# AdaLN-FFN with LoRA experts on one core: the last tile's 656 columns as 236 and 420 instead of 144 and twice 256

## The chip, the cores and the metric

The kernel runs on one core of a Trainium2 chip. The metric is device time in microseconds of one execution, as the median over several runs; less is better. TensorE is called PE below, with its weight loads as PEld; VectorE is DVE, ScalarE ACT, GpSimd POOL and SyncE SP, whose queue issues the loads and stores.

## What is computed

`x` is (64, 32, 512): 64 items of 32 channels by 512 features. Each item picks one of 16 matrices (32 x 32) that mixes its channels, `y`; a linear layer of 512 to 512 with bias follows, with a LoRA delta of the two best of 8 experts, 16 ranks each:

```python
y = einsum('bct,bcd->bdt', x, weights[condition])
result = y @ W_base.T + b_base
logits = y @ W_gate.T                      # 8 experts
route_w = the two largest of softmax(logits), over their sum, at their places, else 0
h = einsum('bnd,erd->bner', y, A)          # 8 experts x 16 ranks
delta = einsum('bner,eor->bno', h * route_w[..., None], B)
out = x + result + delta
```

## The kernel before

**Tiles.** Four items make a tile of 128 rows; there are 16 tiles, 0 to 15 (`LAST`). `x_sb` holds all of them, and each tile's result is added into `x_sb` and stored from there.

**Splitting.** Each fp32 operand is held as a high and a low part, so one product is made of three: `y_hi` with `w_hi`, `y_hi` with `w_lo`, `y_lo` with `w_hi`. With four chunks of 128 features this gives twelve steps for each tile (`ORDER`). The weight side `w_all` has 648 columns: 256 of the base, 64 ranks, 256 of the base, 64 ranks, 8 of the gate. `BASE` is 256, `H` 64, `HALF` 320, `E` 8. The `y` part is the stationary operand and is loaded anew before every product.

**A middle tile** on PE: `mix_tile` (L461, the channel mix of the next tile), then twelve times two products of 320 and 328 columns into the two banks of `main_ps` (`main_step`, L479). Between them stand, for the tile before it, the transpose of `hw`, the weighted ranks (`turn`, L489), and six LoRA products (`lora`, L499).

**The last tile** has no successor to cover its routing. So PE first makes ranks and gate alone: `side_columns` takes 72 + 72 = 144 columns in two runs, twelve products into `y_ps[0]` (L554), and DVE can route (`route_tile`, L356 to L380) while PE makes the base's 512 columns, twelve times two products of 256 (L560). After step 1 stands `turn(14)`, after step 7 `turn(15)` and `lora(14)`. Then comes `lora(15, by_half=True)`: three products for the first half of the columns, then three for the second, each with a signal `base_done`.

**DVE in the last tile** goes in the written order: routing of tile 14, which ends in its `hw` (L376), routing of tile 15, `low_hwT(14)` (L385, the low part of the transposed ranks), the bias of tile 14 (L392), `low_hwT(15)`, the bias of tile 15, the add of tile 14 (L398), then two adds of 256 columns for tile 15 (L442). PE's `lora(t)` waits for `low_hwT(t)`, and its `turn(t)` for `hw` of `t`. ACT makes `hwT_hi` (L279) between the transpose and `low_hwT`.

**SP** issues each tile's store after its add (L209), and for tile 15 two stores of 128 x 256 (L213). At the end it waits for all of them.

Of the kernel before, what the change touches and what calls it, by code (L numbers as in the profile page):

```python
# [5 lines left out]
def adaln_ffn_kernel(  # L6
# [20 lines left out]
    ALU = mybir.AluOpType  # L27
# [9 lines left out]
    E = w_all.shape[1] - D - RANKS  # L37
# [6 lines left out]
    BASE, H, G = OUT // 2, RANKS // 2, E // 2  # L44
    HALF = BASE + H
    ALL = 2 * HALF + E
    SIDE = H + E
    LAST = TILES - 1
# [4 lines left out]
    STEPS = len(ORDER)  # L53
    TURN_AT, LORA_AT = 4, 9
    FIRST_MIX_AT = 6
    LAST_TURN_AT = 1, 7


    WARM_BEFORE, WARM_BESIDE, WARM_BEHIND = (512, 512, 512, 256), (256,), (256, 256, 256)
# [2 lines left out]
    out_tiles = out.rearrange("(t q) c n -> t (q c) n", q=Q)  # L62
# [3 lines left out]
    with ctx:  # L66
# [9 lines left out]
        x_sb = sb("x_sb", [P, TILES, D])  # L76
# [4 lines left out]
        b_hi = sb("b_hi", [P, OUT], f32r)  # L81
        b_lo = sb("b_lo", [P, OUT], f32r)
# [23 lines left out]
        hwT_hi = [sb(f"hwT_hi{i}", [P, P], f32r) for i in range(2)]  # L106
        hwT_lo = [sb(f"hwT_lo{i}", [P, P], f32r) for i in range(2)]
# [9 lines left out]
        y_ps = [ps(f"y_ps{i}") for i in range(2)]  # L117
        main_ps = [ctx.enter_context(nc.psum_tensor(f"main_ps{i}", [P, 2, 512], f32)) for i in range(2)]
# [52 lines left out]
        hwT_lo_ready = sem("hwT_lo_ready")  # L171
        base_done = sem("base_done")
# [3 lines left out]
        def first_halves():  # L176

            for h, bank in enumerate((y_ps[0], hwT_ps[0])):
                f = slice(h * D // 2, (h + 1) * D // 2)
                yield bank[:, 0:D // 2], y_hi[0][:, f], y_lo[0][:, f]  # L180

        block = ctx.enter_context(nc.Block())

        @block.sync
        def _(sp):
            def load_x(t):
                sp.dma_start(x_sb[:, t, :], x_tiles[t, :, :]).then_inc(x_landed[t], 16)

            def load_w(c):
                sp.dma_start(w_raw[:, c, :], w_chunks[c, :, :]).then_inc(w_landed[c], 16)  # L190

            sp.dma_start(cond_sb[:, :], cond).then_inc(cond_landed, 16)
            sp.dma_start(table[:, :, :], cond_w.rearrange("(p k) d -> p k d", k=K)).then_inc(table_landed, 16)
            load_w(0)
            load_w(1)
            load_w(2)
            load_w(3)
            load_x(1)
            sp.dma_start(b_raw[:, :], b_lora).then_inc(b_landed, 16)
            sp.dma_start(bias_sb[:, :], bias.to_broadcast([P, OUT])).then_inc(bias_landed, 16)  # L200
            load_x(2)
            load_x(3)
            for t in range(LAST):
                if t + 4 < TILES:

                    sp.wait_ge(y_done, t + 2)
                    load_x(t + 4)
                sp.wait_ge(result_ready, t + 1)
                sp.dma_start(out_tiles[t, :, :], x_sb[:, t, :]).then_inc(stored, 16)  # L209
            for half in range(2):  # L210
                n = slice(half * BASE, (half + 1) * BASE)
                sp.wait_ge(result_ready, LAST + half + 1)
                sp.dma_start(out_tiles[LAST, :, n], x_sb[:, LAST, n]).then_inc(stored, 16)  # L213
            sp.wait_ge(stored, 16 * (TILES + 1))

        @block.gpsimd
# [89 lines left out]
        def _(dve):  # L306
# [47 lines left out]
            def route_tile(t, h, logits):  # L354
                dve.wait_ge(main_done, t + 1)
                if t >= 1:  # L356
                    dve.wait_ge(second_ready, t)
                dve.max(top[:, :], logits).then_inc(top_ready, 1)  # L358
                dve.wait_ge(top_ready, t + 1)
                dve.max_index(top_ids[:, :], top[:, :], logits).then_inc(ids_ready, 1)  # L360
                dve.wait_ge(ids_ready, t + 1)
                dve.tensor_tensor(one_hot[:, :, :],
                                  expert_ids[:, :].unsqueeze(1).to_broadcast([P, 2, E]),
                                  top_ids[:, 0:2].unsqueeze(2).to_broadcast([P, 2, E]),
                                  ALU.is_equal).then_inc(one_hot_ready, 1)
# [55 lines left out]
            for t in range(1, TILES):  # L421
                before = main_ps[(t - 1) % 2]
                route_tile(t - 1, before[:, :, BASE:HALF], before[:, 1, HALF:HALF + E])
                if t + 2 < TILES:
                    select(t + 2)
                if t == LAST:
                    side = y_ps[0][:, 0:2 * SIDE].rearrange("p (h n) -> p h n", h=2)
                    route_tile(LAST, side[:, :, 0:H], side[:, 1, H:SIDE])
                low_hwT(t - 1)
                if t + 1 < TILES:  # L430
                    low_y(t + 1)
                add_bias(t - 1)
                if t == LAST:
                    low_hwT(LAST)
                    add_bias(LAST)
                finish(t - 1)

            dve.wait_ge(xb_ready, TILES)
            for half in range(2):
                n = slice(half * BASE, (half + 1) * BASE)  # L440
                dve.wait_ge(base_done, LAST + half + 1)
                dve.tensor_tensor(x_sb[:, LAST, n], main_ps[LAST % 2][:, half, 0:BASE], x_sb[:, LAST, n],  # L442
                                  ALU.add).then_inc(result_ready, 1)

        @block.tensor
        def _(pe):
# [20 lines left out]
                y, w = ((y_hi, w_hi), (y_hi, w_lo), (y_lo, w_hi))[n]  # L467
                return y[t % 2][:, c * P:(c + 1) * P], w[:, c, :]

            def side_columns(w):  # L470

                first = w[:, BASE:BASE + SIDE]
                return bass.AP(first.tensor, first.offset, [first.ap[0], [HALF, 2], [1, SIDE]])

            def main_step(t, i, c, n):
                y, w = operands(c, n, t)
                for half in range(2):
# [10 lines left out]
                    pe.wait_ge(hwT_lo_ready, t - 1)  # L488
                pe.transpose(hwT_ps[t % 2][:, 0:P], hw[t % 2][:, :], ident[:, :]).then_inc(hwT_done, 1)  # L489

            def lora(t, by_half=False):
                pe.wait_ge(hwT_lo_ready, t + 1)
                parts = ((hwT_hi, b_hi), (hwT_hi, b_lo), (hwT_lo, b_hi))
                order = [(n, half) for n in range(3) for half in range(2)]
                if by_half:
                    order.sort(key=lambda x: x[1])
                for n, half in order:
                    h, w = parts[n]
                    last = pe.matmul(main_ps[t % 2][:, half, 0:BASE], h[t % 2][:, :],  # L499
                                     w[:, half * BASE:(half + 1) * BASE],  # L500
                                     start=False, stop=n == 2, skip_group_check=True)
                    if (n, half) == order[-1] or by_half and n == 2:
                        last.then_inc(base_done, 1)

            pe.wait_ge(warm_ready, 1)
            warm_up(WARM_BEFORE)
# [41 lines left out]


            pe.wait_ge(y_lo_ready, TILES)  # L550
            side = y_ps[0][:, 0:2 * SIDE].rearrange("p (h n) -> p h n", h=2)
            for i, (c, n) in enumerate(ORDER):
                y, w = operands(c, n, LAST)
                last = pe.matmul(side, y, side_columns(w), start=i == 0, stop=i == STEPS - 1)  # L554
            last.then_inc(main_done, 1)
            pe.wait_ge(result_ready, LAST - 1)
            for i, (c, n) in enumerate(ORDER):
                y, w = operands(c, n, LAST)
                for half in range(2):
                    pe.matmul(main_ps[LAST % 2][:, half, 0:BASE], y, w[:, half * HALF:half * HALF + BASE],  # L560
                              start=i == 0, stop=i == STEPS - 1)
                if i == LAST_TURN_AT[0]:
                    turn(LAST - 1)
                if i == LAST_TURN_AT[1]:
                    turn(LAST)
                    lora(LAST - 1)
            lora(LAST, by_half=True)


# [33 lines left out]
```

## Time and profile before

| | |
|---|---|
| median of 3 runs | 99.46 us (99.31 to 99.56) |
| the profiled execution | 99.65 us, span 97.8 us |
| PE busy, PEld busy | 91.6 us (94%), 88.6 us (91%) |
| DVE, ACT, POOL busy | 64.9 us, 23.7 us, 16.7 us |
| the chain that ended last | PE 89%, DMA 3%, ACT 1%, DVE 1% |
| DMA | 10.67 MB, mean 109 GB/s |

Times in the views count from the start of the span. A product's record in the timeline is longer than its share of the engine, since products are pipelined: the pace is the distance between two starts. The chain of work goes back from the last instruction, at each step to what released it; its rows have start, length, engine, what is written, line and count.

### The profile page before, as it was taken

To read this page: it belongs to the slowest core of one execution; us is meant where nothing else is said; L and a number is where in the kernel's file an instruction comes from. 1 tells how busy PE (TensorE), PEld (TensorE's weight loads), DVE (VectorE), ACT (ScalarE), POOL (GpSimd) and SP (SyncE) were. 2 spreads that over 40 slices of the span, in tenths; PEclk is the share of its full clock that TensorE was granted. 3 is DMA by queue.
4 is the path that set the end of the run, shared out by engine and by line. 5 is a ranking of instruction groups with operands and counts; after the bars stand their busy time and mean duration, and the time that the engine had idled before them with its cause. 6 is when DMAs were issued, how large, how long until landed. Compare 5 with 4: busy or idle time off the path is not lost.

```text
span 97.8 us, 1830 instructions
## 1 busy us (share of the span) xinstructions
PE 91.6 (94%) x652; PEld 88.6 (91%) x652; DVE 64.9 (66%) x228; ACT 23.7 (24%) x56; POOL 16.7 (17%) x30
## 2 busy tenths in 40 slices
PE   4599898999999999999999999999999999999980
PEld 1179788999999999999999999999999999999970
DVE  3453786686767675767768676767576866767880
ACT  5135543131221304040313122130404031311300
POOL 4186033012030303030301203030300000000000
PEclk9999999999999999999999999999999999999999
DMA  1989730033150707060413325060707020302005
GB/s 31 289 291 360 261 94 25 7 116 110 52 173 5 216 0 215 13 188 33 168 53 120 105 77 147 15 209 0 215 16 208 7 107 0 107 7 88 19 4 210
DMA packets 6392, 10.67 MB, mean 109 GB/s; under 512 B 1024, under 2 KB 1648, under 8 KB 6384
## 3 DMA queue, kind: packets, MB, share of 16 engines
q1 hardware_dynamic: 5760, 10.05, 31.9%
q0 software_dynamic: 480, 0.25, 1.0%
q10 hardware_dynamic: 144, 0.26, 0.9%
q8 instruction: 5, 0.08, 0.4%
q14 instruction: 3, 0.02, 0.1%
HBM read 6.37 MB, written 4.19 MB: 108 GB/s over the span
## 4 chain that ended last, share of the span: by engine, by line
PE 89%; DMA 3%; ACT 1%; DVE 1%; issue 1%; POOL 0%; SPq 0%; DVEq 0%; POOLq 0%
PE main_ps L479 54%; PE y_ps L461 15%; PE main_ps L499 11%; PE main_ps L560 3%; DMA table<-cond_w 3%; PE hwT_ps L489 2%; PE hwT_ps L449 1%; PE y_ps L554 1%; PE hwT_ps L461 1%; DVE w_lo L346 1%; ACT w_hi L262 1%; PE main_ps L514 1%; POOL table_split L232 0%; DVE x_sb L442 0%; ACT y_hi L288 0%
## 5 line engine op out<-in xcount | busy, mean ns | idle before, releaser
L479 PE MATMUL main_ps<-w_lo,y_hi 128*128 128x320 f32 x120 | 29.2, 324 | 0.3 <-DVE w_lo L346 0.3
L479 PE MATMUL main_ps<-w_hi,y_hi 128*128 128x320 f32 x120 | 29.3, 325 | 0.0
L479 PE MATMUL main_ps<-w_hi,y_lo 128*128 128x320 f32 x120 | 27.6, 311 | 0.0
L236 POOL DMA_INDIRECT mixw<-cond_w,row_ids x15 | 14.5, 964 | 50.3 <-PE y_ps L461 49.3
L479 PEld LDWEIGHTS main_ps<-w_lo,y_hi 128*128 128x128 f32 x120 | 20.0, 191 | 0.7 <-DVE w_lo L346 0.5
L479 PEld LDWEIGHTS main_ps<-w_hi,y_lo 128*128 128x128 f32 x120 | 20.5, 189 | 0.0
L479 PEld LDWEIGHTS main_ps<-w_hi,y_hi 128*128 128x128 f32 x120 | 19.5, 192 | 0.0
L461 PE MATMUL y_ps<-mix,x_sb 128*128 128x128 f32 x124 | 17.2, 282 | 0.5 <-issue 0.5
L461 PEld LDWEIGHTS y_ps<-mix,x_sb 128*128 128x128 f32 x124 | 16.0, 195 | 1.4 <-issue 1.2
L272 ACT ACTIVATE second<-top 128x1 f32<-128x1 f32 x16 | 4.7, 295 | 44.6 <-DVE top L358 44.6
L398 DVE TENSOR_TENSOR x_sb<-main_ps,x_sb 128x512 f32<-128x512 f32 x15 | 10.4, 691 | 5.8 <-PE main_ps L499 5.8
L385 DVE TENSOR_TENSOR hwT_lo<-hwT_ps,hwT_hi 128x128 fp32r<-128x128 f32 x16 | 4.7, 292 | 13.5 <-ACT hwT_hi L279 13.5
L392 DVE TENSOR_TENSOR x_sb<-x_sb,bias_sb 128x512 f32<-128x512 f32 x16 | 10.9, 683 | 0.0
L268 ACT ACTIVATE y_hi<-y_ps 128x512 fp32r<-128x512 f32 x15 | 9.0, 599 | 7.5 <-PE y_ps L461 7.5
L351 DVE TENSOR_TENSOR y_lo<-y_ps,y_hi 128x512 fp32r<-128x512 f32 x15 | 10.2, 682 | 0.4 <-ACT y_hi L268 0.4
L279 ACT ACTIVATE hwT_hi<-hwT_ps 128x128 fp32r<-128x128 f32 x16 | 4.4, 278 | 11.1 <-issue 6.9
L499 PE MATMUL main_ps<-b_hi,hwT_hi 128*128 128x256 f32 x32 | 6.6, 284 | 0.0
L499 PE MATMUL main_ps<-b_hi,hwT_lo 128*128 128x256 f32 x32 | 6.6, 283 | 0.0
L499 PE MATMUL main_ps<-b_lo,hwT_hi 128*128 128x256 f32 x32 | 6.6, 282 | 0.0
L376 DVE SCALAR_TENSOR_TENSOR hw<-main_ps,weight,route 128x128 f32<-128x128 f32 x15 | 5.3, 351 | 0.5
L499 PEld LDWEIGHTS main_ps<-b_hi,hwT_hi 128*128 128x128 f32 x32 | 5.4, 188 | 0.0
L449 PE MATMUL hwT_ps<-warm 128*128 128x256 bf16 (+1 forms) x11 | 3.8, 473 | 1.5 <-DVE warm L307 1.5
(65 smaller groups left out, 76.2 us busy)
## 6 DMA issues: line engine op xcount, KB each, us to landing
x_sb<-x SPq DMA_DIRECT2D x15, 256.0 KB, 2.8
out<-x_sb SPq DMA_DIRECT2D x15, 256.0 KB
w_raw<-w_all SPq DMA_DIRECT2D x4, 324.0 KB, 3.8
x_sb<-x ACTq DMA_DIRECT2D x1, 256.0 KB, 2.8
b_raw<-b_lora SPq DMA_DIRECT2D x1, 256.0 KB
bias_sb<-bias SPq DMA_DIRECT2D x1, 256.0 KB, 6.8
out<-x_sb SPq DMA_DIRECT2D x2, 128.0 KB
mixw<-cond_w,row_ids POOLq DMA_INDIRECT x15, 2.6
```

Of the source, the lines that this page charges most:

```text
L236: pool.indirect_dma_start(mixw[:, t, :], None, cond_w, bass.IndirectOffsetOnAxis(row_ids[:, t:t + 1], 0))\
L268: act.activation(y_hi[t % 2][:, :], y_ps[t % 2][:, :], ACT.Copy).then_inc(y_hi_ready, 1)
L272: act.activation(second[:, :], top[:, 0:1], ACT.Exp, bias=top[:, 1:2], scale=-1.0)\
L351: dve.tensor_tensor(y_lo[t % 2][:, :], y_ps[t % 2][:, :], y_hi[t % 2][:, :].bitcast(f32), ALU.subtract).then_inc(y_lo_ready, 1)
L376: dve.scalar_tensor_tensor(out=hw[t % 2][:, :].rearrange("p (h e r) -> p h e r", h=2, e=G), in0=h.rearrange("p h (e r) -> p h e r", e=G), ...
L385: dve.tensor_tensor(hwT_lo[t % 2][:, :], hwT_ps[t % 2][:, 0:P], hwT_hi[t % 2][:, :].bitcast(f32), ALU.subtract).then_inc(hwT_lo_ready, 1)
L392: dve.tensor_tensor(x_sb[:, t, :], x_sb[:, t, :], bias_sb[:, :], ALU.add).then_inc(xb_ready, 1)
L398: dve.tensor_tensor(tile, main_ps[t % 2][:, :, 0:BASE], tile, ALU.add)\
L449: pe.matmul(hwT_ps[1][:, 0:n], warm[:, 0:P], warm[:, 0:n], start=True, stop=True)
L461: last = pe.matmul(dst, x_sb[:, t, f], mix[t % 2][:, :, :], start=True, stop=True)
L479: last = pe.matmul(main_ps[t % 2][:, half, 0:n_cols], y, w[:, half * HALF:half * HALF + n_cols], start=i == 0, stop=i == STEPS - 1)
L499: last = pe.matmul(main_ps[t % 2][:, half, 0:BASE], h[t % 2][:, :], w[:, half * BASE:(half + 1) * BASE], start=False, stop=n == 2, skip_gr ...
```

## The change

Only the last tile's columns are grouped in another way. `RUN` is 118, `REST` = 320 + 8 - 118 = 210, `KEPT` = 256 - 210 = 46. The first product of each step now has two runs of 118 columns: 54 of the base and 64 ranks, and 46 of the base, 64 ranks and the gate's 8, together 236, into `y_ps[0]`. The second product of a step has the first 210 columns of each base half, 420, into one bank of `main_ps`. (Eight base columns are made in both.) The last LoRA group, adds and stores follow these parts: first the 420 columns, then the 92 (46 and 46) which stayed in `y_ps[0]`. A store of a part has two runs per row of the output, of 840 bytes, then of 184 bytes, where it had one of 1024.

```diff
+    RUN = 118
+    REST = HALF + E - RUN
+    KEPT = BASE - REST
...
+        def runs(of, start, step, count):
+
+            first = of[:, start:start + count]
+            return bass.AP(first.tensor, first.offset, [first.ap[0], [step, 2], [1, count]])
+
+        def last_parts():
+
+            yield main_ps[LAST % 2][:, 0, 0:2 * REST].rearrange("p (h n) -> p h n", h=2), slice(0, REST)
+            yield runs(y_ps[0], E, RUN - E, KEPT), slice(REST, BASE)
...
-            for half in range(2):
-                n = slice(half * BASE, (half + 1) * BASE)
-                sp.wait_ge(result_ready, LAST + half + 1)
-                sp.dma_start(out_tiles[LAST, :, n], x_sb[:, LAST, n]).then_inc(stored, 16)
+            for part, (_, columns) in enumerate(last_parts()):
+                sp.wait_ge(result_ready, LAST + part + 1)
+                sp.dma_start(out_tiles[LAST, :, :].rearrange("p (h n) -> p h n", h=2)[:, :, columns],
+                             x_sb[:, LAST, :].rearrange("p (h n) -> p h n", h=2)[:, :, columns])\
+                    .then_inc(stored, 16)
...
-                    side = y_ps[0][:, 0:2 * SIDE].rearrange("p (h n) -> p h n", h=2)
-                    route_tile(LAST, side[:, :, 0:H], side[:, 1, H:SIDE])
+                    route_tile(LAST, runs(y_ps[0], RUN - H, RUN - E, H), y_ps[0][:, 2 * RUN - E:2 * RUN])
...
-            for half in range(2):
-                n = slice(half * BASE, (half + 1) * BASE)
-                dve.wait_ge(base_done, LAST + half + 1)
-                dve.tensor_tensor(x_sb[:, LAST, n], main_ps[LAST % 2][:, half, 0:BASE], x_sb[:, LAST, n],
-                                  ALU.add).then_inc(result_ready, 1)
+            for part, (done, columns) in enumerate(last_parts()):
+                tile = x_sb[:, LAST, :].rearrange("p (h n) -> p h n", h=2)[:, :, columns]
+                dve.wait_ge(base_done, LAST + part + 1)
+                dve.tensor_tensor(tile, done, tile, ALU.add).then_inc(result_ready, 1)
...
-                last = pe.matmul(side, y, side_columns(w), start=i == 0, stop=i == STEPS - 1)
+                last = pe.matmul(y_ps[0][:, 0:2 * RUN].rearrange("p (h n) -> p h n", h=2), y,
+                                 runs(w, HALF - RUN, HALF + E, RUN), start=i == 0, stop=i == STEPS - 1)
...
-                for half in range(2):
-                    pe.matmul(main_ps[LAST % 2][:, half, 0:BASE], y, w[:, half * HALF:half * HALF + BASE],
-                              start=i == 0, stop=i == STEPS - 1)
+                pe.matmul(rest, y, runs(w, 0, HALF, REST), start=i == 0, stop=i == STEPS - 1)
...
-            lora(LAST, by_half=True)
+            pe.wait_ge(hwT_lo_ready, LAST + 1)
+            for done, columns in ((rest, rest_columns), (kept, kept_columns)):
+                for n, (h, w) in enumerate(((hwT_hi, b_hi), (hwT_hi, b_lo), (hwT_lo, b_hi))):
+                    last = pe.matmul(done, h[LAST % 2][:, :], w[:, :].rearrange("p (h n) -> p h n", h=2)[:, :, columns],
+                                     start=False, stop=n == 2, skip_group_check=True)
+                last.then_inc(base_done, 1)
```

PE's stream in the last tile, from the end of the side products to the first LoRA products of tile 14. Before:

```order
456 L554 MATMUL y_ps<-w_lo,y_hi 128x144
457 L554 MATMUL y_ps<-w_hi,y_lo 128x144
458 L560 MATMUL main_ps<-w_hi,y_hi 128x256 x2
459 L560 MATMUL main_ps<-w_lo,y_hi 128x256 x2
460 L489 MATMUL hwT_ps<-ident,hw 128x128
461 L560 MATMUL main_ps<-w_hi,y_lo 128x256 x2
```

And after:

```order
456 L557 MATMUL y_ps<-w_lo,y_hi 128x236
457 L557 MATMUL y_ps<-w_hi,y_lo 128x236
458 L564 MATMUL main_ps<-w_hi,y_hi 128x420
459 L564 MATMUL main_ps<-w_lo,y_hi 128x420
460 L498 MATMUL hwT_ps<-ident,hw 128x128
461 L564 MATMUL main_ps<-w_hi,y_lo 128x420
```

The order of steps and transposes is the same; each step has one product less behind the side products.

PE's stream at its end, the last main step and the LoRA products of tile 15. Before:

```order
474 L560 MATMUL main_ps<-w_hi,y_lo 128x256 x2
475 L499 MATMUL main_ps<-b_hi,hwT_hi 128x256
476 L499 MATMUL main_ps<-b_lo,hwT_hi 128x256
477 L499 MATMUL main_ps<-b_hi,hwT_lo 128x256
478 L499 MATMUL main_ps<-b_hi,hwT_hi 128x256
479 L499 MATMUL main_ps<-b_lo,hwT_hi 128x256
480 L499 MATMUL main_ps<-b_hi,hwT_lo 128x256
```

And after:

```order
474 L564 MATMUL main_ps<-w_hi,y_lo 128x420
475 L573 MATMUL main_ps<-b_hi,hwT_hi 128x420
476 L573 MATMUL main_ps<-b_lo,hwT_hi 128x420
477 L573 MATMUL main_ps<-b_hi,hwT_lo 128x420
478 L573 MATMUL y_ps<-b_hi,hwT_hi 128x2x46
479 L573 MATMUL y_ps<-b_lo,hwT_hi 128x2x46
480 L573 MATMUL y_ps<-b_hi,hwT_lo 128x2x46
```

Still three and three products, but of 420 and 92 columns.

## Rows read from the trace of the kernel before

**Rows 1.** The page: span, busy time, clock of each slice, chain by engine

```profile
span 97.8 us, 1830 instructions
...
PE 91.6 (94%) x652; PEld 88.6 (91%) x652; DVE 64.9 (66%) x228; ACT 23.7 (24%) x56; POOL 16.7 (17%) x30
...
PEclk9999999999999999999999999999999999999999
...
PE 89%; DMA 3%; ACT 1%; DVE 1%; issue 1%; POOL 0%; SPq 0%; DVEq 0%; POOLq 0%
```

**Rows 2.** The chain in order of time, last tile: start us, length us, what

```profile
88.32 0.90 PE main_ps L479 x6
...
91.14 1.41 PE main_ps L560 x12
92.55 0.11 PE hwT_ps L489
92.66 0.71 PE main_ps L499 x6
...
94.78 0.42 DVE x_sb L442
```

**Rows 3.** The timeline of PE: start us, length us, engine, line, what, count

```profile
89.12 0.28 PE L554 MATMUL y_ps<-w_lo,y_hi 128*128 128x144 f32 x1
...
90.01 0.28 PE L554 MATMUL y_ps<-w_hi,y_hi 128*128 128x144 f32 x1
...
94.15 0.28 PE L499 MATMUL main_ps<-b_hi,hwT_hi 128*128 128x256 f32 x1
...
94.39 0.28 PE L499 MATMUL main_ps<-b_hi,hwT_lo 128*128 128x256 f32 x1
```

**Rows 4.** DVE's timeline of the last tile, and (last row) its two last adds

```profile
90.28 0.35 DVE L376 SCALAR_TENSOR_TENSOR hw<-main_ps,weight,route 128x128 f32<-128x128 f32 x1
...
91.58 0.35 DVE L376 SCALAR_TENSOR_TENSOR hw<-y_ps,weight,route 128x128 f32<-128x128 f32 x1
91.85 0.28 DVE L385 TENSOR_TENSOR hwT_lo<-hwT_ps,hwT_hi 128x128 fp32r<-128x128 f32 x1
...
93.01 0.29 DVE L385 TENSOR_TENSOR hwT_lo<-hwT_ps,hwT_hi 128x128 fp32r<-128x128 f32 x1 [0.28 <-ACT hwT_hi L279]
...
93.82 0.68 DVE L398 TENSOR_TENSOR x_sb<-main_ps,x_sb 128x512 f32<-128x512 f32 x1
94.78 0.76 DVE L442 TENSOR_TENSOR x_sb<-main_ps,x_sb 128x256 f32<-128x256 f32 x2 [0.28 <-PE main_ps L499]
...
L442 DVE TENSOR_TENSOR x_sb<-main_ps,x_sb x2: 414/419/424, 94.8 to 95.1; 128x256 f32<-128x256 f32 x2
```

**Rows 5.** Timeline: a DVE result and its waiting load; the second transpose

```profile
11.18 0.29 DVE L340 TENSOR_TENSOR mix<-mixw,diag_mask 128x128 f32<-128x128 f32 x1 [0.50 <-DMA mixw<-cond_w,row_ids]
...
11.53 0.19 PEld L461 LDWEIGHTS y_ps<-mix,x_sb 128*128 128x128 f32 x1 [0.19 <-DVE mix L340]
...
92.29 0.14 PEld L489 LDWEIGHTS hwT_ps<-ident,hw 128*128 128x128 f32 x1
92.39 0.27 PE L489 MATMUL hwT_ps<-ident,hw 128*128 128x128 f32 x1
92.39 0.30 PEld L499 LDWEIGHTS main_ps<-b_hi,hwT_hi 128*128 128x128 f32 x2
```

**Rows 6.** SP's queue: tile 14's store, then L213's two (min/median/max ns)

```profile
94.53 0.33 SPq L209 DMA_DIRECT2D out<-x_sb  x1
...
95.23 0.83 SPq L213 DMA_DIRECT2D out<-x_sb  x2
...
L213 SPq DMA_DIRECT2D out<-x_sb x2: 333/393/453, 95.2 to 95.6; - x2
```

**Rows 7.** Stretches of the tail: length, busy time by engine, clock, DMA share, GB/s

```profile
95.30:95.35 0.05, 0.00 (x0) 0.00 (x0) 0.05 (x1) 0.00 (x0) 0.00 (x0) 1.00 0.00 0
95.35:95.40 0.05, 0.00 (x0) 0.00 (x0) 0.05 (x1) 0.00 (x0) 0.00 (x0) 1.00 0.74 287
96.50:96.60 0.10, 0.00 (x0) 0.00 (x0) 0.00 (x0) 0.00 (x0) 0.00 (x0) 1.00 0.37 113
97.05:97.10 0.05, 0.00 (x0) 0.00 (x0) 0.00 (x0) 0.00 (x0) 0.00 (x0) 1.00 0.02 0
97.10:97.80 0.70, 0.00 (x0) 0.00 (x0) 0.00 (x0) 0.00 (x0) 0.00 (x0) 1.00 0.00 0
```

**Rows 8.** DMA queue 1 in 90:91.2, 96.55:97.2 and 2.2:2.75: packets, MB, share

```profile
q1 hardware_dynamic: 127, 0.23, 50.5%
...
q1 hardware_dynamic: 148, 0.13, 60.3%
...
q1 hardware_dynamic: 74, 0.00, 8.7%
```

More of the change, by code:

```diff
@@ L468, in operands @@
                 return y[t % 2][:, c * P:(c + 1) * P], w[:, c, :]
-            def side_columns(w):
-                first = w[:, BASE:BASE + SIDE]
-                return bass.AP(first.tensor, first.offset, [first.ap[0], [HALF, 2], [1, SIDE]])
             def main_step(t, i, c, n):
@@ L489, in turn, with lora @@
                 pe.transpose(hwT_ps[t % 2][:, 0:P], hw[t % 2][:, :], ident[:, :]).then_inc(hwT_done, 1)
-            def lora(t, by_half=False):
+            def lora(t):
                 pe.wait_ge(hwT_lo_ready, t + 1)
[L493 to L503, printed above, removed]
+                for n, (h, w) in enumerate(((hwT_hi, b_hi), (hwT_hi, b_lo), (hwT_lo, b_hi))):
+                    for half in range(2):
+                        last = pe.matmul(main_ps[t % 2][:, half, 0:BASE], h[t % 2][:, :],
+                                         w[:, half * BASE:(half + 1) * BASE],
+                                         start=False, stop=n == 2, skip_group_check=True)
+                last.then_inc(base_done, 1)
             pe.wait_ge(warm_ready, 1)
@@ L550, in _ @@
             pe.wait_ge(y_lo_ready, TILES)
-            side = y_ps[0][:, 0:2 * SIDE].rearrange("p (h n) -> p h n", h=2)
             for i, (c, n) in enumerate(ORDER):
                 y, w = operands(c, n, LAST)
-                last = pe.matmul(side, y, side_columns(w), start=i == 0, stop=i == STEPS - 1)
+                last = pe.matmul(y_ps[0][:, 0:2 * RUN].rearrange("p (h n) -> p h n", h=2), y,
+                                 runs(w, HALF - RUN, HALF + E, RUN), start=i == 0, stop=i == STEPS - 1)
             last.then_inc(main_done, 1)
             pe.wait_ge(result_ready, LAST - 1)
+            (rest, rest_columns), (kept, kept_columns) = last_parts()
             for i, (c, n) in enumerate(ORDER):
                 y, w = operands(c, n, LAST)
-                for half in range(2):
-                    pe.matmul(main_ps[LAST % 2][:, half, 0:BASE], y, w[:, half * HALF:half * HALF + BASE],
-                              start=i == 0, stop=i == STEPS - 1)
+                pe.matmul(rest, y, runs(w, 0, HALF, REST), start=i == 0, stop=i == STEPS - 1)
                 if i == LAST_TURN_AT[0]:
@@ L566, in _ @@
                     lora(LAST - 1)
-            lora(LAST, by_half=True)
+            pe.wait_ge(hwT_lo_ready, LAST + 1)
+            for done, columns in ((rest, rest_columns), (kept, kept_columns)):
+                for n, (h, w) in enumerate(((hwT_hi, b_hi), (hwT_hi, b_lo), (hwT_lo, b_hi))):
+                    last = pe.matmul(done, h[LAST % 2][:, :], w[:, :].rearrange("p (h n) -> p h n", h=2)[:, :, columns],
+                                     start=False, stop=n == 2, skip_group_check=True)
+                last.then_inc(base_done, 1)
 def kernel(**inputs):
```

## The prediction

> **What bounds the kernel now.** I read the page first: TensorE (PE) has work 94% of the span, the chain that ended last is 89% PE, and the clock row is at the full level, 2.4 GHz, in all slices, so no term below is a clock term [rows 1]. A shorter PE stream should shorten the kernel, as long as nothing else ends later. Then the chain in order of time over the last tile [rows 2]: twelve side products, four main products, the transpose of tile 14's `hw`, twelve main products, the transpose of tile 15's, six LoRA products of tile 14, eight main products, three LoRA products of the first half, and then it leaves PE: VectorE's (DVE's) add of the first half at 94.78, ended at 95.20. The profile follows it no further, and 2.6 us of the span are still to come. So I read the tail by itself: SyncE's (SP's) queue [rows 6] and the DMA engines [rows 7]. The question is not only how much PE gets shorter, but how much of it passes the add, the queue and the two stores.
>
> **PE's prices.** From one start to the next: 144 columns take (90.01 - 89.12)/8 = 0.111 us [rows 3]; 256 columns 1.41/12 = 0.118, and 0.71/6 = 0.118 in the LoRA group; 320 and 328 columns (324 on average) 0.90/6 = 0.150 [rows 2]. Between 144 and 256 columns the price hardly moves, and a transpose of 128 columns takes 0.11 too: there the weight load sets the pace. Above, it goes with the columns, 0.46 to 0.47 ns each.
> - **236 columns** are not in the trace. By 0.46 ns a column they would take 0.109, under the floor of 0.111. I take 0.111; the upper bound is 0.118. Group one costs 0 more, at most 12 x 0.007 = 0.08 us. The 92 columns it gains over 144 ride under the weight load.
> - **420 columns** are not there either. From 324 columns on by 0.46: 0.150 + 96 x 0.46 ns = 0.194; I take 0.193. The lower bound is the array's pace at 2.4 GHz, 420/2.4 = 0.175; the upper is two products, 0.235. So a step falls from 0.235 to 0.193, by 0.042, and twelve by 0.51 us. This is the gain the change has to give.
>
> The Trainium skill (TensorE: Matmul & The Clock Gate, Back-to-back issue gap) gives N/2.4 + 2.5 ns for a warm product. This case's 256 columns take 118 ns where that says 109, so the row decides. By the rule 420 columns would take 178 ns, and the forecast below would be some 0.1 us lower, 99.4.
>
> **What of it passes the last tile.** Eight of the twelve steps lie before the transpose of tile 15, so it could start 8 x 0.042 = 0.34 earlier, at 92.05 and not 92.39 [rows 5]. But DVE has its own chain there, without a gap, and the change takes nothing from it: `hw` of tile 15 is done at 91.58 + 0.35 = 91.93, `hwT_lo` of tile 14 at 91.85 + 0.28 = 92.13 [rows 4]. From the end of a DVE result to the weight load that waits for it takes 0.05 (11.18 + 0.29 to 11.53) and from that load to its product 0.10 (92.29 to 92.39) [rows 5].
> - Tile 14's transpose: `hw` is done at 90.28 + 0.35 = 90.63 [rows 4], its load free at 90.68. PE would come by at 90.60 and has a product of 0.19 to cover it: 0.01 at most.
> - Tile 15's transpose: load at 91.98, product at 92.08, not 92.05.
> - LoRA of tile 14: its first load now goes at 92.39 and would come at 92.08; it needs `hwT_lo` and can go at 92.18. PE is held 0.1. From here PE is 0.21 ahead, not 0.34.
> - The six LoRA products are the same, and four steps give 4 x 0.042 = 0.17. The last LoRA group starts 0.38 ahead, at 93.77 instead of 94.15 [rows 3]. Its `hwT_lo` depends on tile 15's transpose: now 93.01 + 0.29 = 93.30, then 0.3 earlier, no wait.
>
> **The last group and the add.** Before, three products of 256 freed the first half: 94.39 + 0.28 = 94.67, and DVE started at 94.78 [rows 3, 4]. Now the first part has 420 columns: the third starts 2 x 0.193 after the first and lasts 0.16 more than its pitch, as 0.28 is 0.118 + 0.16, so 0.35: 93.77 + 0.39 + 0.35 = 94.51. With the same 0.11 DVE starts at 94.62. Its add costs 0.42 us for 256 columns and 0.68 for 512 [rows 4], 1.02 ns a column: 0.59 us for 420. So it ends at 95.21; before, 95.20. **PE's lead is spent**: 0.38 in hand, 0.22 gone in the wider products (0.15 of two pitches, 0.07 of the longer last one), 0.17 in the wider add. DVE is free in time: tile 14's add starts 0.3 earlier with the transpose and ends by 94.2, and its store goes 0.3 earlier too, behind which the last stores stand. The second part (92 columns, 0.25 us) is ready by 95.4: three products at the floor of 0.111 end at 94.9, and the add starts some 0.51 after the first one's.
>
> **The stores.** SP issued the first part at 95.23, busy 0.33, and the second from 95.61, 0.38 later, although its add had ended at 94.78 + 0.76 = 95.54 [rows 4, 6]. Now it issues at 95.24 and 95.61: the small second part cannot go earlier, since SP's pitch sets it. If a store of 256 short rows needs more of SP than one of 128, this grows; the nearest rows are 0.33 and 0.45 for the same form, so 0 to 0.12, and I take 0.
> Then the data. From issue to first packet takes 0.83 (94.53 to 95.36: the DMA share is 0 up to 95.35 and 0.74 after), the last packet is in by 97.09, and 0.7 follow in which nothing moves [rows 6, 7]. Prices per packet and engine, from share x 16 x stretch / packets [rows 8]: 2048 B rows 0.505 x 16 x 1.2/111 = 87 ns, with the 16 tiny completions hardly counting; 1024 B rows 0.603 x 16 x 0.65/129 = 48 ns; 64 B rows 10 ns (0.087 x 16 x 0.55/74). Before, each part was 8 rows of 1024 B an engine, 0.38 us, with slack between them (share 0.37 from 96.50 to 96.60). Now the first is 16 rows of 840 B: on the line between 1024 and 2048 B 41 ns each, 0.66 us, from 96.07 to about 96.8 with the engines' stagger. The second's packets could start at 96.6 and queue until 96.8: 16 rows of 184 B, by the line between 64 and 1024 B 15 ns each, 0.24 us, to 97.04. Bounds: 10 ns and 48 ns, 0.16 and 0.77. So the last packet comes within 0.05 of 97.09.
>
> **Sum.** Span 97.8 + 0.01 (add) + 0 (SP) - 0.04 (data) = 97.8, with up to 0.08 more if 236 columns hold back DVE's routing of tile 15, of which I take 0.03. The profiled execution has 99.65 for a span of 97.8 and lies 0.19 over the median; the same on the median gives **99.5 us**. A measurement of this kernel can tell about 0.3% from no change, 0.3 us.
>
> **The rivals.**
> 1. *Short rows make the last stores long* (slower). 840 B and 184 B rows are new; the trace has no store under 1024 B. If each costs 48 ns like a 1024 B row, the first store takes 0.77, to 96.9, and the second 0.77 more, to 97.65: +0.56, 100.0 us. It passes the bound of 0.3 from 37 ns per 184 B row on ((97.39 - 96.8)/16). For: two rows where one was, both ends off round addresses. Against: 64 B loads at 10 ns. The Trainium skill (DMA: Bandwidth & Descriptors, Specifications) says that under 512 B an engine reads, modifies and writes and misses its line rate; no row here shows such a store.
> 2. *The 420 columns cost as much as two products* (slower), since they are two runs with a gap. Then PE gains 0: the last group starts at 94.15 still, its part is done 2 x 0.235 + 0.35 later, at 94.97, DVE starts at 95.08, and SP issues at 95.70, 0.47 later than now: 99.9 us. Against: the 144 columns are two runs too, and stand at the floor. It is also the case that the change doesn't do what it says.
> 3. *PE's whole gain comes through* (faster). DVE's chain doesn't hold PE and 420 columns go at 0.178: PE is ahead by 0.51 + 12 x 0.015 = 0.69 and starts the last group at 93.46; the part is done 2 x 0.178 + 0.34 later, at 94.16, and 0.11 + 0.59 + 0.03 on the first store is issued, at 94.89, the second at 95.27: both 0.34 earlier, 99.15 us. For: the waits found above are of 0.1 and less. Against: DVE's chain is full from 90.28 to 92.7, and even an ideal PE has to pay the wider add and SP's pitch.
>
> **How the numbers follow.** The cancelling case 0.60, rival 1 with a costlier issue 0.22, rival 2 0.06, rival 3 0.12. Predicted is the first case's 99.5. Faster by over 0.3% 0.12, within 0.3% 0.60, slower 0.28. The range runs from 99.2, just short of rival 3's end, to 99.95, which takes in rival 2 and leaves out the far end of rival 1.
>
> **What would show it.** The 236-column products 0.111 apart and the 420-column ones 0.19; the LoRA group of tile 14 held at 92.2 by DVE's `hwT_lo`; the last LoRA group at 93.8; the first add over 0.58 long and ended at 95.2; two stores issued at 95.24 and 95.6; the last packet at 97.0 to 97.1. A last packet after 97.4 with the issues where they were is rival 1; products 0.23 apart are rival 2; a first store issued before 95.0 is rival 3. A gain elsewhere, before 89 us, would mean that I missed something: not one instruction differs there.

## The result and the profile after

The changed kernel takes **100.68 us** (median of 4 runs, 100.55 to 100.83) against 99.44 us (99.31 to 99.56): ratio 1.0125, interval 1.0104 to 1.0145. It is 1.2 us slower, outside the range. The profiled execution has 100.59 us with a span of 98.8, against 99.65 and 97.8 [rows 1], so the two traces show 0.95 of it; the rest is that the profiled execution before lies 0.21 over its median and the one after 0.09 under its own. In all the traces of this study the first side product (the first of the twelve products that make ranks and gate) starts between 88.5 and 89.2 us, whatever the last tile does. Below, times are therefore often counted from that start, 89.05 in the kernel before and 89.03 after.

The chain of waits of the changed kernel, in order of time, to be read beside [rows 2]:

```profile
89.19 1.34 PE y_ps L557 x12
90.53 0.38 PE main_ps L564 x2
90.91 0.11 PE hwT_ps L498
91.02 1.16 PE main_ps L564 x6
92.18 0.16 PE hwT_ps L498
92.34 0.85 PE main_ps L504 x6
93.19 0.78 PE main_ps L564 x4
93.96 0.60 PE main_ps L573 x3
...
94.65 0.59 DVE x_sb L457
```

A side product of 236 columns takes 1.34/12 = 0.112, a main product of 420 1.16/6 = 0.193. The two held pieces are there: the second transpose has 0.16 instead of 0.11 and the LoRA group 0.85 instead of 0.71. Their loads in the timeline, which answer [rows 5], and the DVE result that the second waits for:

```profile
91.87 0.28 DVE L401 TENSOR_TENSOR hwT_lo<-hwT_ps,hwT_hi 128x128 fp32r<-128x128 f32 x1
92.01 0.14 PEld L498 LDWEIGHTS hwT_ps<-ident,hw 128*128 128x128 f32 x1 [0.18 <-DVE hw L392]
92.02 0.32 PE L498 MATMUL hwT_ps<-ident,hw 128*128 128x128 f32 x1
92.07 0.68 DVE L408 TENSOR_TENSOR x_sb<-x_sb,bias_sb 128x512 f32<-128x512 f32 x1
92.20 0.19 PEld L504 LDWEIGHTS main_ps<-b_hi,hwT_hi 128*128 128x128 f32 x1
...
93.80 0.36 PE L573 MATMUL main_ps<-b_hi,hwT_hi 128*128 128x420 f32 x1
```

Tile 14's `hwT_lo` is done at 92.15, and the load that waits for it goes at 92.20. So PE starts the last LoRA group at 93.80 and not 94.15 [rows 3]. And then the tail, DVE's adds and SP's queue, beside [rows 4, 6]; the last line is the queue's own view with min/median/max in ns:

```profile
94.65 0.59 DVE L457 TENSOR_TENSOR x_sb<-main_ps,x_sb 128x420 f32<-128x420 f32 x1 [0.48 <-PE main_ps L573]
95.17 0.24 DVE L457 TENSOR_TENSOR x_sb<-y_ps,x_sb 128x92 f32<-128x92 f32 x1
95.28 1.27 SPq L227 DMA_DIRECT2D out<-x_sb  x2
...
L227 SPq DMA_DIRECT2D out<-x_sb x2: 609/611/613, 95.3 to 95.9; - x2
```

The first add ends at 95.25, 0.05 after the kernel before. But **SP is busy 0.61 us with each store** instead of 0.33 and 0.45, so the second goes out at 95.93, not 95.61. The stretches of the tail, beside [rows 7] (length, busy times, clock, DMA share, GB/s):

```profile
96.48:96.53 0.05, 0.00 (x0) 0.00 (x0) 0.00 (x0) 0.00 (x0) 0.00 (x0) 1.00 0.00 0
96.53:96.58 0.05, 0.00 (x0) 0.00 (x0) 0.00 (x0) 0.00 (x0) 0.00 (x0) 1.00 0.40 134
97.50:97.58 0.08, 0.00 (x0) 0.00 (x0) 0.00 (x0) 0.00 (x0) 0.00 (x0) 0.50 0.27 42
97.58:98.76 1.18, 0.00 (x0) 0.00 (x0) 0.00 (x0) 0.00 (x0) 0.00 (x0) 0.50 0.00 0
```

The first packet of the first store moves at 96.53, **1.26 us after its issue** instead of 0.85 (0.28 of these 0.41 are SP's own longer time, the rest comes after it); the last packet ends at 97.58 instead of 97.09; and then nothing moves for **1.18 us, where it was 0.73**. (The clock of 0.50, the level of 1.2 GHz, stands in rows where PE has been idle since 94.8; no product is left for it to slow.) The packets themselves are cheap. Queue 1 in the stretches 96.50:97.10 (840 B rows alone) and 97.35:97.60 (184 B rows and the 16 completions), beside [rows 8]:

```profile
q1 hardware_dynamic: 221, 0.19, 94.3%
...
q1 hardware_dynamic: 159, 0.03, 61.2%
```

That is 0.943 x 16 x 0.60/221 = 41 ns for 840 B and 0.612 x 16 x 0.25/159 = 15 ns for 184 B (16 without the tiny completions). The loss in steps, from the first side product on:

| | before | after | lost so far |
|---|---|---|---|
| last LoRA group starts | 5.10 | 4.77 | -0.33 |
| first store issued | 6.18 | 6.25 | 0.07 |
| second store issued | 6.56 | 6.91 | 0.35 |
| its last packet | 8.04 | 8.55 | 0.51 |
| its last completion signal | 8.38 | 9.35 | 0.97 |
| end of the span | 8.77 | 9.74 | 0.97 |

Half a microsecond is lost between issue and packets, and nearly half between the last packet and its completion. The experiments take these two apart.

### The profile page after: what moved, and what is told of

Its sections match the earlier page's. It is cut to its first block, busy times and chain, and to the rows that moved or that the text cites. A ratio compares the mean times of both kernels' runs of the same rounds, so it can differ in the third digit from the quotient of the medians.

```text
span 98.8 us, 1806 instructions
## 1 busy us (share of the span) xinstructions
PE 91.8 (93%) x640; PEld 88.7 (90%) x640; DVE 64.8 (66%) x228; ACT 23.7 (24%) x56; POOL 16.7 (17%) x30
## 4 chain that ended last, share of the span: by engine, by line
PE 91%; DMA 2%; issue 1%; DVE 1%; POOL 0%; SPq 0%; ACT 0%; DVEq 0%; POOLq 0%
PE main_ps L488 56%; PE y_ps L475 15%; PE main_ps L504 11%; DMA table<-cond_w 2%; PE main_ps L564 2%; PE hwT_ps L498 2%; PE hwT_ps L463 1%; PE y_ps L557 1%; PE hwT_ps L475 1%; PE main_ps L573 1%; DVE x_sb L457 1%; PE main_ps L518 1%; POOL table_split L248 0%; SPq L207 0%; ACT table_split L299 0%
## 5 line engine op out<-in xcount | busy, mean ns | idle before, releaser
L504 PE MATMUL main_ps<-b_hi,hwT_hi 128*128 128x256 f32 x30 | 6.1, 285 | 0.0
L504 PE MATMUL main_ps<-b_hi,hwT_lo 128*128 128x256 f32 x30 | 6.0, 283 | 0.0
L504 PE MATMUL main_ps<-b_lo,hwT_hi 128*128 128x256 f32 x30 | 6.0, 282 | 0.0
```

## The experiments

Points in time of two digits before the point are from the start of the span, those of one digit from the start of the first side product; "late" is the time from a store's last packet to its last completion signal, from the records of the packets and signals in one profiled execution of each run. The kernel before was timed again beside each group of runs (medians 99.50 to 99.58), and a ratio is to those.

**Are the stores the whole of it?** The changed kernel with one store of tile 15:

```diff
-            for part, (_, columns) in enumerate(last_parts()):
-                sp.wait_ge(result_ready, LAST + part + 1)
...
+            sp.wait_ge(result_ready, LAST + 2)
+            sp.dma_start(out_tiles[LAST, :, :], x_sb[:, LAST, :]).then_inc(stored, 16)
```

> The changed kernel with its products and adds as they are, but one store of 128 rows of 2048 B for tile 15 after the second add. Theory S (the loss lies in the form of the last two stores): the adds end at 95.4 as in the changed kernel, SP issues at 95.44 and is busy 0.33, the first packet comes 0.83 later at 96.27, the last by 97.1, the completion 0.35 after that; span 97.8, 99.4 to 99.6 us. Rival P (something in the regrouped products, adds or their memory places costs the 1.2 us): it stays above 100.3 us.

99.59 us, ratio to before 1.0005 (0.9988 to 1.0021). SP's queue shows the store busy 0.33:

```profile
95.34 0.33 SPq L226 DMA_DIRECT2D out<-x_sb  x1
```

The last packet comes at 8.05 and the completion 0.35 after it. The regrouped products, the banks, the adds are as in the changed kernel, and the loss is gone. Rival P falls: it is the two stores.

**The two-run form.** In the changed kernel the two runs lie 256 columns apart in the output, half of a row of 512, so the output side is one list of 256 equal rows (the trace's record of the transfer has 1 x 256 pieces of 840 B there, and 2 x 128 pieces in `two_runs`), while the SBUF side has 128 partitions with two runs. `two_runs` has two runs too, but 384 apart:

```diff
...
+            sp.wait_ge(result_ready, LAST + 2)
+            sp.dma_start(out_tiles[LAST, :, 128:384], x_sb[:, LAST, 128:384]).then_inc(stored, 16)
+            def outer(of):
+                first = of[:, 0:128]
+                return bass.AP(first.tensor, first.offset, [first.ap[0], [384, 2], [1, 128]])
+            sp.dma_start(outer(out_tiles[LAST, :, :]), outer(x_sb[:, LAST, :])).then_inc(stored, 16)
```

> The kernel before, with the last two stores cut in another way, both issued after the second add (95.57 instead of 95.23 and 95.61): first columns 128 to 383 as 128 rows of 1024 B, then columns 0 to 127 and 384 to 511 as two runs of 512 B per partition, whose two output runs do not lie at a stride that lets them merge into 256 equal rows. All rows at multiples of 512 B. Theory F1 (two runs per partition cost SP's time as such): the second store has SP busy 0.61 and its first packet 1.26 after its issue; 16 rows of 28 ns an engine; about 100.1 us. Theory F2 (only the form in which the output counts as one list of 256 rows against 128 partitions costs it): SP busy 0.33 to 0.45 and the first packet at 0.85 to 1.0, about 99.8 us. Completion 0.35 after the last packet in both.

99.88 us, ratio 1.0032 (1.0019 to 1.0045). The plain store and the two-run store in SP's queue:

```profile
95.45 0.33 SPq L211 DMA_DIRECT2D out<-x_sb  x1
95.83 0.44 SPq L215 DMA_DIRECT2D out<-x_sb  x1
```

0.44 is what a plain second store has too (0.45 in the kernel before), and its first packet moves 0.97 after its issue, as the second store's did before (0.96). So two runs cost SP nothing in this place, and F1 falls. (`contig` below has such a store in the first place, with 0.39 and 0.92 where a plain one has 0.33 and 0.85: a small part may be the two runs'. The time of `two_runs` is longer than before since both its stores wait for the second add.) `run200` has rows of 512 B in the merged form:

```diff
-    RUN = 118
+    RUN = 200
```

> The changed kernel with RUN = 200: both stores have two runs of 128 columns, 512 B rows at multiples of 512 B; side products of 400 columns (0.185 us each instead of 0.111, 0.9 us more before tile 15's routing), main products of 256. To be read in the trace, not by the time (100.5 to 101.3): SP busy 0.61 for each store and 1.26 to the first packet (form). Theory A: completion 0.35 after the last packet. Rival F or the count of 256 rows: 0.7 to 0.8.

100.37 us in one execution. SP is busy 0.61 and 0.63 with its two stores, the first packet comes 1.27 after the issue, and the last store is 0.35 late:

```profile
L227 SPq DMA_DIRECT2D out<-x_sb x2: 613/620/626, 95.3 to 96.0; - x2
```

So the merged form costs a first store 0.28 us of SP and 0.41 from issue to first packet (the 0.28 included), with rows of 512, 832 and 840 B, at round addresses or not; second stores of 184 and 192 B show the same 0.61 and 1.26. It is not what makes the completion late. Every kernel with this form shows it (the changed one, `run120` and `run200`) and none of the others; what in the making of the transfer takes the time was not tried.

**The late completion.** `cut250` has plain stores with a cut off round addresses:

```diff
-                n = slice(half * BASE, (half + 1) * BASE)
+                n = slice(0, 250) if half == 0 else slice(250, OUT)
```

> The kernel before, with the two last stores cut at column 250 instead of 256: 128 rows of 1000 B, and 128 rows of 1048 B which begin 1000 B into the row. The form with 128 rows stays. Theory A (the late completion, 0.80 us after the last packet instead of 0.35, comes from rows that begin or end off a round address): SP and the start as before (0.33 busy, 0.83 to the first packet), completion 0.7 to 0.8 after the last packet, 99.8 to 99.9 us. Rival F (it comes from the form with two runs per partition): completion at 0.35, 99.4 to 99.5 us.

99.59 us, ratio 1.0013 (1.0001 to 1.0025). The first store (1000 B) is 0.60 late, the second (1048 B) 0.38, and the second sets the end: neither what theory A nor what rival F said. The late completion needs no two-run form, but not every odd edge makes it.

`run120` moves the changed kernel's edges to multiples of 64 B, and four columns from the 420 to the 236 with them; the stores keep their form and their points of issue (6.23 and 6.89 for 6.25 and 6.91):

```diff
-    RUN = 118
+    RUN = 120
```

> The changed kernel with RUN = 120 instead of 118: rows of 832 B and 192 B, which begin and end at multiples of 64 B; products of 240 and 416 columns. SP's issue stays at 0.61 and the first packet at 1.26 by all theories. Theory A with 64 B as the unit: completion falls from 0.80 to 0.35 after the last packet, about 100.1 us. Theory A with a larger unit, or rival F: it stays at 0.7 to 0.8, 100.6 us.

> The same kernel as run120, timed: the changed kernel with rows of 832 and 192 B at multiples of 64 B. Theory: form alone 0.6 to 0.75 us over before, so 100.1 to 100.25 us, and 0.4 to 0.5 under the changed kernel. If the first look was luck, 100.6.

100.24 in one execution; timed, 100.09 us, ratio 1.007 (1.0048 to 1.0091), 0.6 under the changed kernel. SP's queue, and the stretch after the last packet:

```profile
95.11 1.27 SPq L227 DMA_DIRECT2D out<-x_sb  x2
```

```profile
97.41:98.13 0.72, 0.00 (x0) 0.00 (x0) 0.00 (x0) 0.00 (x0) 0.00 (x0) 0.50 0.00 0
```

SP's part is all there (1.27 for two issues), the last packet comes at 8.53 (changed kernel 8.55), and then 0.72 us pass, not 1.18. The rows have 832 and 192 B, so what is late is not that rows are short or two to a partition. What went with the lateness is that the rows had an edge at 840 B.

`small_plain` has odd edges and short rows in plain stores, `swap250` the order of `cut250` turned around, `cut248` the edge at 32 B, `cut402` and `cut456` short rows with an odd and a 32 B edge:

```diff
-            for half in range(2):
-                n = slice(half * BASE, (half + 1) * BASE)
+            for half, n in ((0, slice(0, 256)), (1, slice(256, 466)), (1, slice(466, OUT))):
```

```diff
-            for half in range(2):
-                n = slice(half * BASE, (half + 1) * BASE)
-                sp.wait_ge(result_ready, LAST + half + 1)
+            sp.wait_ge(result_ready, LAST + 2)
+            for n in (slice(250, OUT), slice(0, 250)):
```

```diff
-                n = slice(half * BASE, (half + 1) * BASE)
+                n = slice(0, 248) if half == 0 else slice(248, OUT)
```

`cut402` and `cut456` are the last edit with their own column, and both stores after the second add.

> The kernel before, with its second half stored by two stores of 128 rows: 840 B that begin at 1024 and end off a multiple of 64 B, and 184 B that begin there and end at 2048. So the short and off-address rows without the two-run form, and one store more (SP's pitch of 0.38 to 0.5). Theory A (completion is late where rows begin or end within a 64 B block): SP 0.33 to 0.45 for each, the last packet at 97.2, completion 0.6 to 0.8 after it: 99.9 to 100.0 us. Rival (lateness needs the 256 rows of the two-run form too): completion 0.35 to 0.4, 99.6 to 99.7 us.

> The kernel before, with the two last stores cut at column 248: rows of 992 B and of 1056 B, at a multiple of 32 B but not of 64 B. The run with the cut at column 250 had the first store's completion 0.60 after its last packet and the second's 0.38, where 0.42 and 0.34 stood with the cut at 256. If blocks of 64 B are the unit, the first store's completion comes at 0.55 to 0.65 again; if 32 B are, at 0.42.

> The kernel before, with the cut at column 250 and both stores after the second add, columns 250 to 511 first, then 0 to 249. If rows that end off a multiple of 64 B are what completes late, the second store now completes 0.6 or more after its last packet and the first at 0.4; if the one that comes first of two which share a 64 B block is late, the first at 0.6 and the second at 0.38 as before. Issues at 95.57 and 95.95, 99.8 to 100.0 us.

> The kernel before, with both last stores after the second add: 128 rows of 1608 B, then 128 rows of 440 B that begin 1608 B into the output row, off a multiple of 32 B, and end at its end. Open is what makes a store's completion late: rows of 184 B that begin off were late (0.77 after the last packet), rows of 1048 B that begin off were not (0.38). Theory B (a row that begins off is late if it is short): the second store 0.6 to 0.8. Theory C (late only if the odd piece lies in the row's last 256 B block, which the end at 2048 and the start at 1608 are not): 0.38. The first, which ends off, 0.6 or more in both. Issues at 95.57 and 95.95; 99.7 us by C, 100.0 by B.

> The same with the cut at column 456: rows of 1824 B and of 224 B, all edges at multiples of 32 B, the middle one not of 64 B. If 32 B are the unit for short rows too, both completions come 0.34 to 0.40 after the last packet; if a short row needs 64 B, the second's comes at 0.6 to 0.8.

| run | us | first store: bytes, odd edge, late | second: bytes, odd edge, late |
|---|---|---|---|
| before | 99.44 | 1024, none, 0.36 | 1024, none, 0.35 |
| changed | 100.68 | 840, end, 0.71 | 184, start, 0.80 |
| run120_timed | 100.09 | 832, none, 0.40 | 192, none, 0.35 |
| cut248 | 99.67 | 992, none (32 B), 0.37 | 1056, none (32 B), 0.38 |
| cut456 | 99.92 | 1824, none (32 B), 0.38 | 224, none (32 B), 0.47 |
| cut250 | 99.59 | 1000, end, 0.60 | 1048, start, 0.38 |
| swap250 | 100.03 | 1048, start, 0.37 | 1000, end, 0.78 |
| small_plain | 100.31 | 840, end, 0.66 | 184, start, 0.77 |
| cut402 | 100.34 | 1608, end, 0.51 | 440, start, 0.95 |

The times of `cut248`, `cut456`, `swap250` and `cut402` are of one execution each; those with other points of issue than before (`cut456`, `swap250`, `cut402`, and the three stores of `small_plain`) are to be read by the "late" columns. The row of `small_plain` leaves out its first store, one of 1024 B rows with 0.36.

"Odd" is off a multiple of 32 B; every odd edge here lies 8 B past such a multiple. Every store without an odd edge, in the other runs too, is 0.34 to 0.47 late; of ten with one, eight are 0.51 to 0.95 and two, the 1048 B rows that start odd, 0.37 and 0.38. (Where two stores overlap, the sixteenth signal after the packets is taken for the first one.) `small_plain` has the lateness without the two-run form, 0.77 against 0.35, and ends 0.66 later than the kernel before, of which 0.24 is a later last packet. An edge at a multiple of 32 B is enough: `cut248` has its edge there and no lateness (64 B as the unit falls), and `cut456` says the same of short rows, with 0.47 a little above the others. A smaller unit, 16 B, was not tried. Nor do these runs tell apart what always came together: a row with an odd edge in the output also has it in SBUF, its length is odd too, and its neighbour across the edge is the other store, in flight at the same time. "Odd edge" stands for all of them here. Theory C falls with cut402: its odd edge does not lie in the row's last 256 B block, and the store is later than any. Its packets are gone early, and then nothing moves to the end:

```profile
97.16:97.21 0.05, 0.00 (x0) 0.00 (x0) 0.00 (x0) 0.00 (x0) 0.00 (x0) 1.00 0.07 18
97.22:98.54 1.32, 0.00 (x0) 0.00 (x0) 0.00 (x0) 0.00 (x0) 0.00 (x0) 1.00 0.00 0
```

Theory B (an odd start is late in short rows) fits 184, 440 and 1048 B, but where between 440 and 1048 B it turns, and why, stays open. `swap250` says that the odd end is late in the second place too, and there it sets the end: 9.53 against 9.09 in `cut456`, whose stores are issued at the same points (0.13 of that is the later last packet, 0.31 the completion). That the store with the odd end is late in both orders (0.60, 0.78), and the 1048 B one in neither, shows that the order doesn't decide it.

**Does the regrouping gain anything?** `whole` gave 99.59 with PE ahead by 0.34 at the last LoRA group, and still held at step 7. With tile 15's transpose one step later:

```diff
-    LAST_TURN_AT = 1, 7
+    LAST_TURN_AT = 1, 8
```

> The run with one whole store of tile 15, and besides tile 15's transpose and tile 14's LoRA after step 8 instead of step 7. Theory: PE's hold of 0.1 at these two, which waits for the vector engine's hw and hwT_lo, is gone, so the last LoRA group starts 0.1 earlier after the side products' first start (4.67 instead of 4.77 us), and the store goes 0.1 earlier: 99.4 to 99.5 us. If the hold is not that wait, the distance stays at 4.77.

> The same kernel as whole_turn8 (regrouped products, tile 15's transpose after step 8, one whole store), timed: in the first look its end lay 8.62 us after the first side product, 0.15 earlier than in the kernel before. Theory: 0.10 to 0.2 us faster, a ratio of 0.998 to 0.999, hardly to be told from before.

99.42 in one execution; timed, **99.34 us, ratio 0.9977 (0.9962 to 0.9992)**: 0.2 us faster than the kernel before, within the 0.3 us that the prediction took for no change, but with an interval clear of 1. Its chain:

```profile
90.92 1.35 PE main_ps L561 x7
92.28 0.11 PE hwT_ps L495
92.39 0.71 PE main_ps L501 x6
93.10 0.58 PE main_ps L561 x3
93.68 0.60 PE main_ps L570 x3
```

The transpose is back at 0.11 and the LoRA group at 0.71; the last group starts at 4.59 where `whole` has 4.76 and the kernel before 5.10, more than the 4.67 expected: the whole 0.51 of the narrower products is there. The hold was the wait for DVE, and moving the pair by one step undoes it.

`best` keeps two plain stores of 1024 B rows as before and the transpose after step 8, and makes the 92 columns' LoRA before the last main step so that their add is early:

```diff
+            for half in range(2):
+                tile = x_sb[:, LAST, half * BASE:half * BASE + REST]
+                dve.tensor_tensor(tile, rest[:, half, :], tile, ALU.add).then_inc(result_ready, 1)
...
+                if i == STEPS - 2:
+                    pe.wait_ge(hwT_lo_ready, LAST + 1)
+                    last_lora(*parts[0])
+            last_lora(*parts[1])
```

> What the findings point to: products of 236 and 420 columns as in the changed kernel, tile 15's transpose after step 8, the LoRA products of the 92 kept columns before the last main step and their add early, then the 420 columns' LoRA, two adds of 210 columns, and two stores of 128 rows of 1024 B as in the kernel before. Theory: first store issued at 95.1 and second at 95.46 (before 95.23 and 95.61), last packet at 96.95, completion 0.35 later: 99.3 us, 0.1 to 0.2 under before. Rival (the regrouping gains nothing even with plain stores): 99.5.

99.41 us, ratio 0.999 (0.9979 to 1.0001): the stores went out at 6.11 and 6.49 (6.18 and 6.56 before), half of the lead that I had worked out, and the end lies 0.08 earlier; in the times that cannot be told from no change.

`contig` moves the weights so that the kept columns lie in the middle of the output: two runs that do not merge, all edges at 64 B. The transpose stands after step 8 here too, and the products have 232 and 416 columns.

```diff
-            yield main_ps[LAST % 2][:, 0, 0:2 * REST].rearrange("p (h n) -> p h n", h=2), slice(0, REST)
-            yield runs(y_ps[0], E, RUN - E, KEPT), slice(REST, BASE)
+            yield (main_ps[LAST % 2][:, 0, 0:2 * REST].rearrange("p (h n) -> p h n", h=2),
+                   lambda of: runs(of, 0, REST + 2 * KEPT, REST))
+            yield runs(y_ps[0], 0, RUN - KEPT, KEPT), lambda of: runs(of, REST, KEPT, KEPT)
```

> The changed kernel with another layout of the weight columns (base half 0, ranks 0, gate, ranks 1, base half 1), so that the last tile's side product is one run of 232 columns and the 96 kept base columns lie in the middle of the output: the first store has two runs of 208 columns per partition (832 B) whose output side does not merge into a list of 256 rows, the second 128 rows of 384 B; all at multiples of 64 B. Tile 15's transpose stands after step 8. Theory: SP busy 0.33 and 0.45 instead of 0.61 twice, first packets 0.85 and 1.0 after the issues, completion 0.35 after the last packet; the end lies 8.55 to 8.65 us after the first side product (before 8.77, changed kernel 9.74); 99.2 to 99.4 us. If two runs cost SP's time without the merge too, SP is busy 0.61 with the first store and the end lies at 8.9 or later, 99.6 us.

99.48 us, ratio 0.9994 (0.9979 to 1.0009). SP is busy 0.39 and 0.49, the first packet comes 0.92 after the issue, both stores are 0.39 late, and the end lies at 8.66 instead of 9.74:

```profile
L233 SPq DMA_DIRECT2D out<-x_sb x1: 388/388/388, 94.8 to 94.8; - x1
...
L236 SPq DMA_DIRECT2D out<-x_sb x1: 492/492/492, 95.3 to 95.3; - x1
```

With nearly the same split of the work over PE and DVE, the two causes taken away give back the 1.2 us (these stores are issued 0.2 and 0.5 earlier than the changed kernel's, partly by the transpose's move); the gain over the kernel before is again too small to measure.

## Why the prediction was wrong

**Right, by its own steps.** 236 columns at the floor: 0.112 for 0.111. 420 columns: 0.193, as taken; the Trainium skill's rule (TensorE: Matmul & The Clock Gate, Back-to-back issue gap), which the page gives for a single isolated product and the prediction applied to a stream, would give 0.178, and the row says 0.193. DVE's hold: the load for tile 14's LoRA at 92.20 for 92.18. The last LoRA group at 93.80 for 93.77, the add 0.59 long and ended at 95.25 for 95.21. That PE's lead is spent in the wider last products and the wider add: the changed kernel's first add ends 0.05 later than before, and `whole`, with the same products and adds, gains nothing. The packets: 41 and 15 ns, as interpolated. Rival 2 and rival 3 are out.

**The step that failed is "The stores".** Three of its terms were taken over from stores of another form.
- *"0 to 0.12, and I take 0"* for SP: it was 0.28 more for the first store and 0.16 for the second. The nearest rows, 0.33 and 0.45, were all of one form, 128 rows for 128 partitions, and so bounded nothing. The prediction itself named the new form, "a store of 256 short rows", and had no row for it. Effect on the second issue: 0.35 (0.07 for the later first issue, 0.28 for the pitch).
- *Issue to first packet*, 0.83 before and taken as fixed: 1.26. The second store waited 0.96 before (95.61 to 96.57) and 1.26 after, 0.3 more; its shorter data, 0.38 instead of 0.52, gave back the half, and the last packet came 0.51 later.
- *"0.7 follow in which nothing moves"*, also taken as fixed: 1.18. Late completion, 0.80 for 0.35, half of the loss.

**Rival 1 had the right side and the wrong mechanism.** It put the price on the packets, up to 48 ns each, and its point of decision at 37 ns; they cost 15. The sentence of the Trainium skill beside it (DMA: Bandwidth & Descriptors, Specifications: under 512 B an engine reads, modifies and writes) does not explain the late completion by length: rows of 192 B complete 0.35 after the last packet, rows of 1000 and 1608 B with an odd end 0.60 and 0.51. The packets show no step at 512 B either, 27 ns for 440 B and 28 for 512, though a short row does carry fewer bytes per ns (184 in 16, 1024 in 48). The same page of the Trainium skill (How a descriptor splits into AXI transactions) describes pieces cut at 256 B addresses, with beats of 32 B. That edges at 32 B are not late in these runs agrees with the beat, but no run shows that the beat is why, and `cut402` is late with an edge outside the last 256 B block. "Both ends off round addresses" stood in the rival's text and deserved a term of its own.

The range should have reached further up: with no row of such a store, the upper bound of three terms was missing, and only one of them, SP's, was asked about at all.

The measured 1.2 us are nearly 0.3 more than the two traces show, since each profiled execution lies off its median. `run120_timed` has the same sign (0.6 us over before, 0.5 in the traces). Up to the last tile the two traces agree (89.05 and 89.03); whether the late completion varies from execution to execution is open.

## What to carry to other kernels

A store's cost is not its packets alone: the time the queue's engine takes to issue it, the time to its first packet and the time from its last packet to its completion each depend on its form, and at a kernel's end all three are on the path. Before splitting an output differently, ask which form the transfer will have, keep the output side to one row per partition (or a stride that doesn't merge), and keep every edge at a multiple of 32 B, where no store here was late. And a faster engine gains only what the slowest of its partners lets through: here 0.51 us of TensorE became 0.33 at the last group and 0 at the store, until the transpose and the LoRA products behind it were moved by a step: then 0.51 at the last group and 0.2 at the end.

## What the runs showed that I had not expected

- A store whose output side is one list of 256 rows against 128 partitions with two runs: SP busy 0.61 us instead of 0.33 (0.45 for a second store), first packet 1.26 us after the issue instead of 0.85, in all three kernels with it, with rows of 184 to 840 B. Two runs at a stride that doesn't merge: 0.39 and 0.92 as the first store, 0.44 and 0.97 as the second.
- Odd edges (8 B past a multiple of 32 B; edge in the output, edge in SBUF, length and neighbour not told apart): the last completion signal 0.51 to 0.95 us after the last packet in eight of ten stores, instead of 0.34 to 0.47, at packet prices that stay the same (1000 B 48 ns, 1024 B 48 ns).
- A row's packet costs by its length, with no step and whatever its edges: 184 B 16 ns, 384 B 25 ns, 512 B 28 ns, 840 B 41 ns per packet and engine.
